# Layer 1 of a two-layer fused kernel: where the product with C runs, where the gated input stands, and which engine sums the step size

## The reference, cut to what matters

```python
x_dbl = einsum('kd,bdl->bkl', x_proj_w, xs)            # xs: after conv and silu
dts, Bs, Cs = x_dbl[:, :6], x_dbl[:, 6:10], x_dbl[:, 10:]
delta = softplus(einsum('dr,brl->bdl', dt_w, dts) + dt_b)
log_dA = maximum(delta * A, log(1e-9))
P = exp(cumsum(log_dA))
dB_u = delta * Bs * xs
hs = P * cumsum(dB_u / maximum(P, 1e-9))
y = einsum('bdnl,bnl->bdl', hs, Cs) + xs * Ds
```

## Time and profile before

| | us |
|---|---|
| median of 3 runs | 4415.92 (4414.74 to 4424.39) |
| profiled execution | 4400.48 |
| its span | 4398.7 |
| busy in the span: PE, DVE, ACT, POOL | 3939.3, 3451.4, 2840.9, 1851.3 |
| mean granted TensorE clock | 0.916 |

### The profile page before, as it was taken

How to read it: one execution, slowest core, us unless ns; L and a number is a source line. 1 busy time by engine, 2 the same in 40 slices (tenths; PEclk the granted TensorE clock), 3 DMA queues, 4 the chain that set the end, 5 groups by cost and what they waited for, 6 DMA issues and landing times.

```text
span 4398.7 us, 75925 instructions
## 1 busy us (share of the span) xinstructions
PE 3939.3 (90%) x23254; PEld 2822.9 (64%) x23254; DVE 3451.4 (78%) x5147; ACT 2840.9 (65%) x4727; POOL 1851.3 (42%) x2001
## 2 busy tenths in 40 slices
PE   6999999999999898978988989989889899899887
PEld 6777787878787878675655555645555556465332
DVE  3766666675758484805998989989989899899899
ACT  1544545362727181747878878887788887888765
POOL 0322323141414051403655645645556556455554
PEclk9999999999999999988998989989989889899776
DMA  7555564646373734284434324424334244142000
GB/s 231 143 167 163 149 180 125 192 109 216 99 231 95 234 94 165 75 180 101 102 77 93 99 63 108 112 53 104 91 77 109 59 109 115 48 110 83 17 17 19
DMA packets 315032, 507.54 MB, mean 115 GB/s; under 512 B 190144, under 2 KB 255392, under 8 KB 314288
## 3 DMA queue, kind: packets, MB, share of 16 engines
q1 hardware_dynamic: 314576, 502.08, 42.7%
HBM read 424.94 MB, written 77.07 MB: 114 GB/s over the span
## 4 chain that ended last, share of the span: by engine, by line
issue 19%; DVE 17%; PE 11%; ACT 6%; POOL 2%; DVEq 1%; DMA 0%; SPq 0%; ACTq 0%; POOLq 0%
DVE ps_q L944 11%; PE ps_front L1144 3%; DVE u L966 3%; PE ps_y L1219 2%; DVE u L951 2%; POOL u L881 1%; DVE q_last L957 1%; PE ps_c L1194 1%; ACT d_a L1043 1%; ACT d_a L1049 1%; ACT xs L1007 1%; PE ps_front L1137 1%; PE ps_prep L1175 1%; PE ps_y L1216 1%; PE ps_b L1194 1%
## 5 line engine op out<-in xcount | busy, mean ns | idle before, releaser
L881 POOL TENSOR_TENSOR u<-dxs,b_rows 128x448 f32<-128x448 f32 x672 | 765.3, 1139 | 167.0 <-DVE u L966 163.6
L1219 PE MATMUL ps_y<-hc,ident 128*128 128x448 f32 x1344 | 730.7, 629 | 0.0
L966 DVE TENSOR_TENSOR_SCAN u<-d_a,h_last,u 128x448 f32<-128x448 f32 x576 | 695.6, 1208 | 0.0
L1043 ACT ACTIVATE d_a<-delta,log_eps,a_neg 128x448 f32<-128x448 f32 x672 | 507.0, 755 | 270.8 <-DVE u L966 263.9
L293 POOL TENSOR_TENSOR ln_rstd<-ln_var,minus_half 112x7 f32<-112x7 f32 x128 | 248.9, 1944 | 999.6 <-DVE ln_var L372 999.6
L944 DVE TENSOR_TENSOR_SCAN ps_q<-d_a,q_last,ps_q 128x448 f32<-128x448 f32 x576 | 659.9, 1146 | 0.0
L537 PE MATMUL ps_stage<-win,taps 124*112 124x112 f32 x6144 | 610.8, 261 | 19.3 <-issue 16.2
L537 PEld LDWEIGHTS ps_stage<-win,taps 124*112 124x112 f32 x6144 | 609.6, 179 | 21.8 <-issue 21.8
L1144 PE MATMUL ps_front<-win,taps 120*112 120x112 f32 x4608 | 584.5, 281 | 6.1 <-ACT win L1000 3.7
L1144 PEld LDWEIGHTS ps_front<-win,taps 120*112 120x112 f32 x4608 | 518.3, 189 | 85.4 <-issue 84.7
L471 ACT ACTIVATE act_h<-ps_up,b 128x448 f32<-128x448 f32 x672 | 411.3, 635 | 225.2 <-PE ps_up L564 225.0
(11 more groups left out here) (99 smaller groups left out, 7573.6 us busy)
## 6 DMA issues: line engine op xcount, KB each, us to landing
taps<-in_t_dram SPq DMA_DIRECT2D x192, 896.0 KB, 5.7
taps<-in_t_dram SPq DMA_DIRECT2D x192, 672.0 KB, 5.8
xres<-in_x_dram SPq DMA_DIRECT2D x224, 168.0 KB, 2.5
x_dram<-x1o SPq DMA_DIRECT2D x224, 168.0 KB, 2.0
x1pad<-x_dram SPq DMA_DIRECT2D x96, 392.0 KB, 8.8
out_dram<-y SPq DMA_DIRECT2D x168, 224.0 KB
xpad<-in_x_dram SPq DMA_DIRECT2D x29, 1176.0 KB, 10.5
conv<-in_x_dram SPq DMA_DIRECT2D x3, 1176.0 KB, 15.9
```

The lines of the kernel that those rows point to most:

```text
L881: nc.gpsimd.tensor_tensor(u[s % U_SLOTS][:, :], dxs[:, t, :], b_rows[n][:, :], ALU.mult).then_inc(u_done, 1)
L966: nc.vector.tensor_tensor_scan(u[s % U_SLOTS][:, :], d_a[s % DA_SLOTS][:, :], u[s % U_SLOTS][:, :], first, ALU.mult, ALU.add).then_inc(h_d ...
L1043: nc.scalar.activation(d_a[s % DA_SLOTS][:, :], delta[:, t, :], ACT.Relu, bias=log_eps[:, 0:1], scale=a_neg[:, t, n:n + 1]).then_inc(clipp ...
L1219: mm = nc.tensor.matmul(ps_y[:, 0:BT], ident[:, :], hc[s % 2][:, :], start=False, stop=(n == N - 1))
```

## The change

Five things in layer 1:

- The product with C moves from DVE to POOL (`times_c`), in place in the state buffers h, of which there are 4 (`H_SLOTS`). The C rows are no longer spread once a step, but 4 times a band into a bank shared with the B rows (ps_bc), and kept in SBUF by ACT (`keep_c`).
- The gate writes its result over q in PSUM. There are two ps_q banks, used in turn, and the state scan reads the gated input from PSUM and writes h in SBUF. u is free after the gate, and has 3 buffers.
- The copy of the state's last column moves from POOL to DVE (`keep_h`), into spare columns of the first ps_q bank.
- delta is summed by DVE in one instruction, max(z, 0) + Ln, with z read from PSUM; ACT's Relu of softplus goes. The bias of z comes in by a constant row of the matmul.
- `add_y` stands two steps behind (`Y_LAG`) instead of one. The SiLU block of j = 9 in the last band moves to j = 10, and the transposes that feed it from j = 8 and 9 to j = 9 and 10. The sums of delta stand at DVE's steps 7, 9, 11 (7, 8, 9 in the last band).

```diff
-ZSTEPS = 4
-U_SLOTS = 4
-U_AHEAD = U_SLOTS - 1
+ZSTEPS = 3
+U_SLOTS = 3
+U_AHEAD = U_SLOTS
+H_SLOTS = 4
+Y_LAG = 2
+Z_SLOTS = 2
...
-        ps_b = pb("ps_b")
-        ps_q = pb("ps_q")
-        ps_c = pb("ps_c")
+        ps_bc = pb("ps_bc")
+        ps_q = [pb(f"ps_q{i}") for i in range(2)]
         ps_y = pb("ps_y")
+        no_q = ps_q[0][:, BT:BT + 1]
+        h_last = ps_q[0][:, BT + 1:BT + 1 + STEPS]
...
+        SUM_AT = [(7, 9, 11)] * (BANDS - 1) + [(7, 8, 9)]
+        DXS_AT = (8, 10, 11)
...
+        SPREAD_B_AT, KEEP_B_AT = (6, 7, 8, 9), (7, 8, 9, 10)
+        SPREAD_C_AT, KEEP_C_AT = (10, 11), (11,)
+        SPREAD_C_NOW, KEEP_C_NOW = {0: 2, 1: 3}, {0: 1, 1: 2, 2: 3}
+        def z_bank(b, t):
+            return ps_front[0] if b == 0 and t == 2 else ps_prep[(1 + t) % 2]
...
-            def times_b(g, s):
+            def times_b(g, s, first=False):
                 b, t, n = s // STEPS, s % STEPS // N, s % N
                 if t == 0:
                     pool.wait_ge(b_kept, g * B_UNITS + b * N + n + 1)
-                if U_SLOTS <= s < U_SLOTS + KEPT:
-                    pool.wait_ge(h_kept, g * KEPT + s - U_SLOTS + 1)
                 if n == 0:
                     pool.wait_ge(dxs_ready, g * RUNS + s // N + 1)
+                if not first:
+                    pool.wait_ge(gated, g * S + s - U_SLOTS + 2)
                 nc.gpsimd.tensor_tensor(u[s % U_SLOTS][:, :], dxs[:, t, :], b_rows[n][:, :],
                                         ALU.mult).then_inc(u_done, 1)
+            def times_c(g, s):
+                b, t, n = s // STEPS, s % STEPS // N, s % N
+                if t == 0:
+                    pool.wait_ge(c_kept, g * B_UNITS + b * N + n + 1)
+                pool.wait_ge(h_done, g * S + s + 2)
+                if b + 1 < BANDS:
+                    pool.wait_ge(h_kept, g * KEPT + s + 1)
+                nc.gpsimd.tensor_tensor(h[s % H_SLOTS][:, :], h[s % H_SLOTS][:, :], c_rows[n][:, :],
+                                        ALU.mult).then_inc(hc_done, 1)
...
                     prepare = more or b + 1 < BANDS
+                    if s > 0:
+                        times_c(g, s - 1)
                     if prepare and j == SPLIT_AT:
                         split(f, fb)
-                    if prepare and j in SUM_AT:
-                        sum_delta(f, fb, SUM_AT.index(j))
-                    if prepare and j - 1 in SUM_AT:
-                        times_x(f, fb, SUM_AT.index(j - 1))
-                    pool.wait_ge(h_done, g * S + s + 2)
-                    if b + 1 < BANDS:
-                        add(h_last[:, j:j + 1], u[s % U_SLOTS][:, BT - 1:BT], zeros[:, 0:1]).then_inc(h_kept, 1)
+                    if prepare and j in DXS_AT:
+                        times_x(f, fb, DXS_AT.index(j))
                     if s + U_AHEAD < S:
                         times_b(g, s + U_AHEAD)
                     elif more:
                         times_b(g + 1, s + U_AHEAD - S)
-                    if prepare and j == STEPS - 1:
-                        times_x(f, fb, TILES - 1)
+                times_c(g, S - 1)
...
+            def sum_delta(f, b, t, first=False):
+                n = f * RUNS + b * TILES + t + 1
+                dve.wait_ge(z_step, n * ZSTEPS)
+                if not first:
+                    dve.wait_ge(d_a_ready, (f * BANDS + b - 1) * STEPS + (t + 1) * N)
+                    dve.wait_ge(dxs_ready, n - TILES)
+                nc.vector.scalar_tensor_tensor(delta[:, t, :], z_bank(b, t)[:, 0:BT], 0.0, z_log[t % Z_SLOTS][:, :],
+                                               ALU.max, ALU.add).then_inc(delta_ready, 1)
             def scan_q(g, s):
                 b, j = s // STEPS, s % STEPS
                 dve.wait_ge(d_a_ready, g * S + s + 1)
-                dve.wait_ge(gated, g * S + s + 1)
-                if s > 0:
-                    dve.wait_ge(q_kept, g * KEPT + min(s, KEPT))
+                dve.wait_ge(h_done, g * S + max(s, 1))
+                if s > 1:
+                    dve.wait_ge(q_kept, g * KEPT + min(s - 1, KEPT))
                 first = q_first[:, 0:1] if b == 0 else q_last[:, j:j + 1]
-                nc.vector.tensor_tensor_scan(ps_q[:, 0:BT], d_a[s % DA_SLOTS][:, :],
-                                             ps_q[:, BT:BT + 1].broadcast_to([128, BT]), first,
+                nc.vector.tensor_tensor_scan(ps_q[s % 2][:, 0:BT], d_a[s % DA_SLOTS][:, :],
+                                             no_q.broadcast_to([128, BT]), first,
                                              ALU.mult, ALU.add).then_inc(q_done, 1)
-            def gate(g, s):
-                dve.wait_ge(q_done, g * S + s + 1)
-                dve.wait_ge(u_done, g * S + s + 1)
-                nc.vector.scalar_tensor_tensor(u[s % U_SLOTS][:, :], ps_q[:, 0:BT], 1.0, u[s % U_SLOTS][:, :],
-                                               ALU.min, ALU.mult).then_inc(gated, 1)
-            def keep_q(s):
+            def keep_q(g, s):
                 b, j = s // STEPS, s % STEPS
                 if b + 1 < BANDS:
-                    nc.vector.tensor_copy(q_last[:, j:j + 1], ps_q[:, BT - 1:BT]).then_inc(q_kept, 1)
+                    dve.wait_ge(q_done, g * S + s + 1)
+                    nc.vector.tensor_copy(q_last[:, j:j + 1], ps_q[s % 2][:, BT - 1:BT]).then_inc(q_kept, 1)
+            def gate(g, s):
+                b = s // STEPS
+                dve.wait_ge(q_done, g * S + s + 1)
+                if b + 1 < BANDS:
+                    dve.wait_ge(q_kept, g * KEPT + s + 1)
+                dve.wait_ge(u_done, g * S + s + 1)
+                nc.vector.scalar_tensor_tensor(ps_q[s % 2][:, 0:BT], ps_q[s % 2][:, 0:BT], 1.0, u[s % U_SLOTS][:, :],
+                                               ALU.min, ALU.mult).then_inc(gated, 1)
             def scan_h(g, s):
                 b, j = s // STEPS, s % STEPS
                 dve.wait_ge(gated, g * S + s + 2)
+                dve.wait_ge(y_added, g * S + s + 1)
                 first = zeros[:, 0:1]
                 if b > 0:
                     dve.wait_ge(h_kept, g * KEPT + s - STEPS + 1)
                     first = h_last[:, j:j + 1]
-                nc.vector.tensor_tensor_scan(u[s % U_SLOTS][:, :], d_a[s % DA_SLOTS][:, :], u[s % U_SLOTS][:, :], first,
+                nc.vector.tensor_tensor_scan(h[s % H_SLOTS][:, :], d_a[s % DA_SLOTS][:, :], ps_q[s % 2][:, 0:BT], first,
                                              ALU.mult, ALU.add).then_inc(h_done, 1)
-            def times_c(g, s):
-                dve.wait_ge(h_done, g * S + s + 2)
-                dve.wait_ge(c_ready, g * S + s + 1)
-                nc.vector.tensor_tensor(hc[s % 2][:, :], u[s % U_SLOTS][:, :], ps_c[:, 0:BT], ALU.mult).then_inc(hc_done, 1)
...
+            def keep_h(g, s):
+                b, j = s // STEPS, s % STEPS
+                if b + 1 < BANDS:
+                    dve.wait_ge(h_done, g * S + s + 2)
+                    nc.vector.tensor_copy(h_last[:, j:j + 1], h[s % H_SLOTS][:, BT - 1:BT]).then_inc(h_kept, 1)
...
                 for s in range(S):
+                    b, j = s // STEPS, s % STEPS
+                    f, fb = next_band(g, b)
+                    keep_q(g, s)
                     gate(g, s)
-                    keep_q(s)
                     if s > 0:
-                        times_c(g, s - 1)
+                        keep_h(g, s - 1)
+                    if (more or b + 1 < BANDS) and j in SUM_AT[b]:
+                        sum_delta(f, fb, SUM_AT[b].index(j))
                     if s + 1 < S:
                         scan_q(g, s + 1)
                     scan_h(g, s)
-                times_c(g, S - 1)
...
+                z = z_log[t % Z_SLOTS][:, :]
                 if late:
-                    act.wait_ge(z_step, n + 3)
-                    nc.scalar.activation(z_log[:, t, :], z_log[:, t, :], ACT.Ln, bias=1.0).then_inc(z_step, 1)
+                    act.wait_ge(z_step, n + 2)
+                    nc.scalar.activation(z, z, ACT.Ln, bias=1.0).then_inc(z_step, 1)
                     return
                 act.wait_ge(z_done, f * RUNS + b * TILES + t + 1)
-                if not first:
-                    act.wait_ge(delta_ready, f * RUNS + (b - 1) * TILES + t + 1)
-                src = ps_prep[(1 + t) % 2][:, 0:BT]
-                nc.scalar.activation(z_log[:, t, :], src, ACT.Abs, bias=bias).then_inc(z_step, 1)
-                nc.scalar.activation(z_pos[:, t, :], src, ACT.Relu, bias=bias).then_inc(z_step, 1)
-                act.wait_ge(z_step, n + 2)
-                nc.scalar.activation(z_log[:, t, :], z_log[:, t, :], ACT.Exp, scale=-1.0).then_inc(z_step, 1)
+                if t >= Z_SLOTS:
+                    act.wait_ge(delta_ready, f * RUNS + b * TILES + t - Z_SLOTS + 1)
+                elif not first:
+                    act.wait_ge(delta_ready, f * RUNS + b * TILES)
+                nc.scalar.activation(z, z_bank(b, t)[:, 0:BT], ACT.Abs).then_inc(z_step, 1)
+                act.wait_ge(z_step, n + 1)
```

(18 more changed lines are left out.)

149 lines of the change are left out of this document (80 added, 69 removed).

## The result

The changed kernel takes 4369.14 us (median of 4 runs, 4360.68 to 4374.16); the kernel before, beside it, 4416.82 (4414.74 to 4424.39). The ratio is 0.9896, 95% interval [0.9874, 0.9919]: 1.0% faster, where 4185 (4090 to 4310) was forecast. The profiled execution took 4369.61, its span is 4367.8, the mean granted clock 0.918.

A forecast was written before the change was run, and what follows sets the result against it. VectorE was taken to set the pace, with TensorE close behind. 203 us less VectorE work plus 24 less idle made 227 off the profiled 4400.5, 4173.5; the median lies 15.4 higher, 4189, stated as 4185 (4090 to 4310).

The forecast's parts named there:

- VectorE's own work: VectorE's busy time in layer 1: 251.8 us a group, 2014 for eight groups against 2217.4, 203 less.
- The dependent copy: VectorE's keep_q, which the gate now waits for: 0.23 us a step, bounds 0.15 to 0.28.
- the contention: VectorE's state scan slowed beside GpSimd's products: 59 us over 672 scans, forecast to go altogether.
- Rival 3: Slower: GpSimd still blocks VectorE's scans that read SBUF, 289 us more, 4474; chance 4%.
- The loads of the others: Busy times in layer 1: GpSimd 31.9 and TensorE some 34.3 us a band, ScalarE about 243 a group.
- Rival 4: Slower: TensorE falls to its low clock more often, granted 0.70 in the bands, 4491; chance 5%.
- That makes 16 us a group where there were 19.6: VectorE's idle time in layer 1: 128 us over eight groups where 152.3 stood, 24 less.
- the turn: From one group to the next: VectorE waits for ScalarE behind its SiLU blocks, 10 us a turn.
- The 6 for Ln: Middle bands: VectorE's sum of delta waits for ScalarE's Ln, 6 us a group, half of 11.5.
- My own bound: Sign of being wrong, at VectorE's sum of delta: it waits over 10 us a group.
- the ring over ps_y: Not forecast; later theory: with one ps_y bank, TensorE waits for ScalarE's copy of y, ScalarE for TensorE's convolution.
- Rival 1: ScalarE sets the pace in layer 1: idle 30 us a group, 115 us less, 4300; chance 20%.

The follow-up runs named there:

- 4708 us: The changed kernel with ScalarE's copy of y moved to the end of its step, behind the row copies, Exp and softplus: 4708.27 us, ratio 1.0678.

## Why the prediction was wrong

- **VectorE's own work: right.** Forecast 2014 us, measured 1987.3. The dependent copy was sized a little high: 0.17 us start to start, not 0.23, so 576 x 0.06 = 35 us too much. The gate into PSUM took 0.54, the upper of its bounds (0.50 to 0.54), where 0.52 was used, and the contention went whole (mean 1127 ns, longest 1.15 us), as the earlier trace rows and the Trainium skill's SBUF — State Buffer, "SBUF: two separate sides", had it. Rival 3 is out.
- **The loads of the others: right.** Per band GpSimd was forecast at 31.9 us and has 30.7, TensorE at 34.3 and has 32.7; ScalarE per group at 243 and has 233.8. That last one is partly luck: the Exp became 0.08 us shorter with its bias as a number (84 x 0.08 = 7 us a group), which the prediction hadn't seen. GpSimd waits for VectorE 354.7 us and is covered. Rival 4 is out as a cause of its own: the clock in layer 1 is 0.88 as before, and in the last group 0.72 for 0.69. It did fall in the band behind a turn: 0.74 in the middle group, where the kernel before had 0.80.
- **The step that failed: "That makes 16 us a group where there were 19.6".** VectorE's idle time is 352.3 us, 44 a group. The 16 were 6 for the middle bands and 10 for the turn; measured are 14.6 and 29.6. The 6 for Ln were read from the earlier trace rows, and alone in the kernel before they measure 5.2. But that trace's lateness of ScalarE was taken as given while the step under it became 0.3 us shorter and the order on TensorE turned. Measured: 22 a group for Ln, 11 for d_a. My own bound stood there ("if the sum waits over 10 us a group"). With the copy of y first, the middle bands idle 6.6, as forecast, so there it was the ring over ps_y that the sum lacked.
- **Why I missed it.** The change also turns the order within TensorE's step: before, the front piece stood ahead of add_y, now add_y stands ahead of it. I gave that no price. (Which of the two closed the ring, this order or the shorter step, no run separates.) So what waits for the copy of y now holds up the convolution, while on ScalarE that copy stays behind clip and front copy in the same step. I compared loads and looked for slack in VectorE's waits; I didn't follow the single-buffered bank from its last reader to its next writer.
- **The turn, the larger part of the miss.** Forecast 10 us, measured 29.6 (19.9 in the first band, 9.7 in the last); by the same measure the kernel before had 16.0. SiLU was sized well (blocks of 7.4 and 8.0 us), but behind the second one come the last copy of y, which waits for TensorE, and the loop's turn, and then the late Lns of the first band. With the ring open, idle time is still 30 us a group, 23.3 of it here: 13 over the forecast. The table loads are 4 of the 23. How the rest divides among the blocks themselves, the order behind them and the low clock of the first band isn't settled by any of these runs.
- **Rival 1** named the engine, ScalarE, and 30 us a group (4300), but as a matter of load. The load is the same at 4251, 4369 and 4708 us.

With the copy of y first the kernel is at 4251, inside the range, and 66 above the forecast; in layer 1 that is 110 us more idle time than forecast, nearly all of it at the turn (8 x 13 = 104), and 34 less work. So of the 184 us between forecast and result (4369 - 4185) the ring accounts for 111 to 118; the rest is the turn, less what the work was below the forecast.

## What to carry to other kernels

When a step gets shorter, list every buffer that has no second copy and is handed between two in-order queues, and write down what stands in front of the instruction that frees it, and what stands behind the one that waits. Here ScalarE, busy for 77% of layer 1, and TensorE, busy for 84%, held each other up; the sign is that each has long waits for the other while neither's busy time grew. Put the instruction that frees a single buffer at the head of its step: here two lines were worth 2.5%, more than the whole change had brought. It is something to try, not a law: the same move gave 0.35% in the kernel before, and row copies put ahead of the front copy cost 54 us.

## What the runs showed beyond that

- The length of a wait tells little of what it costs. TensorE's 260 us of waits for C rows became 235 us, and the kernel 54 us slower. And a sum that comes a step later took 14 us off the wait for Ln and nothing off the time.
- A copy of 128 x 1 that waits for the scan before it, with a gate that waits for the copy, costs 0.17 us start to start, which is what the extra dependent hop within VectorE costs here.
- TensorE's clock can fall within a band. Seven microseconds behind the first stand shown above, PE in the order of time, and then the busy time of the stretch with its granted clock (the third number from the end):

```profile
2739.48 1.01 PE L1275 MATMUL ps_y<-h,ident 128*128 128x448 f32 x2 [1.59 <-ACT win L1035]
2740.33 2.17 PE L1193 MATMUL ps_front<-win,taps 120*112 120x112 f32 x12
```

```profile
2740.30:2742.60 2.30, 2.30 (x14) 2.27 (x13) 1.76 (x3) 1.00 (x2) 1.77 (x2) 0.57 0.03 7
```

  Behind a wait of 1.59 us for ScalarE half a convolution takes 2.17 us, where it took 1.34 at 2733.51 (the earlier trace rows had 1.43 and 2.58). The granted clock was 0.57 in this stretch, most of it at the lower level of 1.2 GHz, and 1.00 in the 13 us before it. That the stall brought the fall is not shown: with the copy of y first TensorE waits 1.59 us at the same place (2701.75), and its granted clock stays at 1.00 for the 10 us behind it.
- An Exp over 128 x 448 took 573 ns with its bias as a number and 655 ns with it read from SBUF. With 672 of them that is 55 us of ScalarE's time in layer 1.
- The best version, the copy of y first with one SiLU block or with two (0.9631 and 0.9644), beats the kernel before by 3.6 to 3.7% and the changed one by 2.5 to 2.7%.
